# Attention steps in two runs of key tiles, with the next projection and the transposed maxima in front of the last values

## The chip, the cores and the metric

The kernel runs on one core of a Trainium2 chip. The metric is the time of one execution on the device in microseconds (us). A step below is one pair of heads against one block of 512 queries; there are 16.

## What is computed

One decoder block over 2048 rows of 256: a recurrent layer, cross attention against 1601 context rows with 8 heads of 64, and a mixture of 16 experts with a shared one, each followed by a normalisation of the rows. The change touches only the attention:

```
q = (x @ Wq).reshape(b, n, HEADS, DIM_HEAD)      # k, v likewise from the context
scores = einsum('bhnd,bhmd->bhnm', q, k) * scale
attn = softmax(scores, axis=-1)
out = einsum('bhnm,bhmd->bhnd', attn, v).reshape(b, n, HIDDEN)
x = layernorm(x + out @ Wo + bo)
```

## The kernel before

`attention` works through 4 chunks of 512 queries (`CHUNKS`), each with 4 pairs of heads (`PAIRS`): step `S` is chunk `S // 4`, pair `S % 4`. The 1601 keys are 13 tiles (`KT`), the last of 65.

For each tile, `score` on TensorE makes the scores of both heads, keys on partitions, in one of two PSUM buffers `st`. It takes four parts, each one matmul for each head: three products of high and low halves of Q and K, and a fourth that adds the negated row maxima (`ones_r` against `M`). The heads lie on partitions 0 to 63 and 64 to 127 of the operands. ScalarE's `exp` (L630) turns the buffer into a tile of `probs` in SBUF, a ring of `RING` places. GpSimd adds the 13 tiles to `accG` (L607). `values` (L816) multiplies a tile of probabilities with V and accumulates in the bank `av`; `sums` (L833) adds `accG` over its partitions into the bank `misc`; `copy_av` moves `av` to `o_raw`, and VectorE's `divide` in four parts (L689 and L691) makes `oT`.

The row maxima of a step are found one step ahead. `q_proj(S+1)` (L761) projects into `misc`, ScalarE's `q_high` and VectorE's `q_low` split it, and 26 pieces (`PIECES`, 13 for each head) of queries against keys go to the banks `mx[0]` and `mx[1]` (L780), one for each head. VectorE reduces each piece (L674; the two short ones of 66 keys L671); piece n waits until the reduction of piece n-2 has emptied its bank. `all_maxima` joins them in `nm`, `max_transpose` (L749) turns them into `mx[1]`, and VectorE's `max_rows` (L659) writes `M`.

At the first step of a chunk, `output` multiplies the last chunk's `oT` with Wo in two halves of 16 matmul passes (L847), `residual` adds x, and in the step behind it `statistics`, GpSimd's `inverse` and ScalarE's `norm` (L640) normalise.

Each engine runs its instructions in the order in which they are written out, and waits only on semaphores. TensorE's order in a step is: transpose of the maxima, projection for the next step, then three rounds of a run of tiles (`RUNS`: 0 to 4, 5 to 8, 9 to 12) and a group of values (`VALUES`: 0 to 2, 3 to 8, 9 to 12). The sums of the step before stand behind the first run. A tile has four slots of scores; `PIECE_AT` says for tiles 1 to 12 in which of then five slots the piece of head 0 and that of head 1 stand. The last pair of pieces (`LATE_PAIR`) stands inside the last group of values, in front of tile 10. `DIVIDE_AFTER` says behind which piece VectorE makes each of the four divides, `SHORT` which pair of pieces is the short one.

Of the kernel before, what the change touches and what calls it, by code (L numbers as in the profile page):

```python
# [13 lines left out]
S, D = 2048, 256  # L14
# [4 lines left out]
KT = (KEYS + P - 1) // P  # L19
# [3 lines left out]
PAIRS = HEADS // 2  # L23
QC = 512
CHUNKS = S // QC
QT = QC // P
# [9 lines left out]
def before_attention(nc, io, mem):  # L36
# [5 lines left out]
    with ExitStack() as ctx:  # L42
# [322 lines left out]
        def _(pe):  # L365
# [81 lines left out]
PIECES = 2 * PIECE_PAIRS  # L447
# [1 line left out]
DIVS = 4  # L449
LAST_V = (3, 5, 7, 9, 11, 12)  # L450
G_ADDS = KT - 1
RUNS = (range(0, 5), range(5, 9), range(9, KT))
HIGH, LOW_QUERY, LOW_KEY, MAXIMA = range(4)
VALUES = (range(0, 3), range(3, 9), range(9, KT))
PIECE_AT = {1: (0, 1), 2: (1, 2), 3: (2, 3), 4: (3, 4), 5: (0, 1), 6: (1, 2), 7: (2, 3), 8: (3, 4),
            9: (0, 1), 10: (0, 1), 11: (1, 2), 12: (2, 3)}
SHORT = 8
LATE_PAIR = 10
DIVIDE_AFTER = (8, 8, 16, 16)
SEEN = {3: 4, 5: 6, 7: 8, 9: 10, 11: 12}  # L460
NORM_AFTER = 4
RING = 8


def at_least(engine, semaphore, count):
# [5 lines left out]
def attention(nc, io, mem):  # L471
# [12 lines left out]
    with ExitStack() as ctx:  # L484
# [124 lines left out]
        @block.scalar  # L609
        def _(act):  # L610
            def q_high(F):
                act.wait_ge(p_q, F)
                at_least(act, p_qk, 2 * (F - 1) * KT)
                act.activation(Q_hi[F % 2][:], misc[:], ACT.Copy).then_inc(a_hi, 1)

            def exp(S, t):
                g, r = S * KT + t, rows_of(t)
                act.wait_ge(p_qk, 2 * (g + 1))
                if g >= RING:
                    act.wait_ge(p_pv, g - RING + 1)  # L620
                    before, old = divmod(g - RING, KT)
                    if before == STEPS - 1:
                        if old in LAST_V:
                            act.wait_ge(v_add, LAST_V.index(old) + 1)
                        else:
                            alone = [k for k in range(1, KT) if k not in LAST_V]
                            act.wait_ge(g_add, before * G_ADDS + alone.index(max(old, 1)) + 1)
                    else:
                        act.wait_ge(g_add, before * G_ADDS + max(old, 1))
                act.activation(probs[0:r, place(S, t)], st[g % 2][0:r, :], ACT.Exp, scale=DH ** -0.5).then_inc(a_probs, 1)  # L630

            def copy_av(S):
                act.wait_ge(p_pv, (S + 1) * KT)
                at_least(act, v_o, S * DIVS)
                act.activation(o_raw[:], av[:], ACT.Copy).then_inc(a_av, 1)

            def norm(c):
                act.wait_ge(g_shift3, c + 1)
                for i in range(QT):
                    act.activation(x1[:, i], x1[:, i], ACT.Identity, bias=shift3[:, i:i + 1], scale=rstd3[:, i:i + 1]  # L640
                                   ).then_inc(a_x2, 1)

            for S in range(STEPS):
                c, p = divmod(S, PAIRS)
                if S > 0:
                    copy_av(S - 1)
                if S + 1 < STEPS:
                    q_high(S + 1)
                for t in range(KT):
                    exp(S, t)  # L650
                    if p == 1 and t == NORM_AFTER and c > 0:
                        norm(c - 1)
            copy_av(STEPS - 1)

        @block.vector
        def _(dve):
            def max_rows(S):
                dve.wait_ge(p_mT, S + 1)
                dve.tensor_tensor(M[:].rearrange("p (i q) -> p i q", i=QT), mx[1][:, 0:P].unsqueeze(1).to_broadcast([P, QT, P]),  # L659
                                  mask[:].unsqueeze(2).to_broadcast([P, QT, P]), ALU.mult).then_inc(v_mT, 1)  # L660

            def q_low(F):
                dve.wait_ge(a_hi, F)
                dve.tensor_tensor(Q_lo[F % 2][:], misc[:], Q_hi[F % 2][:].bitcast(F32), ALU.subtract).then_inc(v_lo, 1)
# [42 lines left out]

            dve.tensor_tensor(mask[:], ident[:, 0:QT], ident[:, DH:DH + QT], ALU.add).then_inc(v_mask, 1)
            dve.wait_ge(v_mask, 1)
            for S in range(STEPS):  # L710
                c, p = divmod(S, PAIRS)
                max_rows(S)
                if p == 1 and c > 0:
                    statistics(c - 1)
                if S + 1 < STEPS:
                    q_low(S + 1)
                    for n in range(1, PIECES + 1):
                        piece_maximum(S + 1, n)
                        for i, at in enumerate(DIVIDE_AFTER):
                            if n == at and S > 0:  # L720
                                divide(S - 1, i)
                        if n == PIECES - 2 and p == 0 and c > 0:
                            residual(c - 1, 0, misc)
                            residual(c - 1, 1, misc)
                    all_maxima(S + 1)
                    if p == 0 and c > 0:
                        residual(c - 1, 2, mx[0])
                        residual(c - 1, 3, mx[0])
            for i in range(DIVS):
                divide(STEPS - 2, i)  # L730
            for n, t in enumerate(LAST_V):
# [14 lines left out]
        def _(pe):  # L746
# [4 lines left out]
            def q_proj(F):  # L751
                c, pair = divmod(F, PAIRS)
                at_least(pe, v_o, (F - 2) * DIVS)
                if pair == 2 and c > 0:
                    pe.wait_ge(v_r, (c - 1) * QT + 2)
                if F == 1:
                    pe.wait_ge(d_wq, 16)
                if pair == 0:
                    pe.wait_ge(d_x1Tc, c * 16)
                for k in range(DK):  # L760
                    mm = pe.matmul(misc[:], wq[:, k, pair * P:(pair + 1) * P], x1T[:, k, :],  # L761
                                   start=(k == 0), stop=(k == DK - 1))
                mm.then_inc(p_q, 1)

            def piece(F, n):

                i, j = piece_of(n)
                h, (k0, kn) = (n - 1) % 2, MC[j]
                rows = slice(DH * h, DH * h + DH)
                if n == 1:  # L770
                    pe.wait_ge(a_hi, F)
                    c, p = divmod(F - 1, PAIRS)
                    if p == 1 and c > 0:
                        pe.wait_ge(v_r, c * QT)
                if n <= 2:
                    at_least(pe, v_mx, (F - 2) * PIECES + PIECES - 2 + n)
                if n > 2:
                    pe.wait_ge(v_mx, (F - 1) * PIECES + n - 2)
                for a, q in enumerate(range(QT) if i is None else (i,)):
                    mm = pe.matmul(mx[h][:, a * kn:(a + 1) * kn], Q_hi[F % 2][rows, q * P:(q + 1) * P],  # L780
                                   K_hi[rows, F % PAIRS, k0:k0 + kn], start=True, stop=True)
                mm.then_inc(p_mx, 1)
# [54 lines left out]
            def output(c, half):  # L837

                if half == 0:
                    pe.wait_ge(d_wo, 16)  # L840
                    pe.wait_ge(v_o, (c + 1) * PAIRS * DIVS)
                else:
                    pe.wait_ge(v_mx, ((c + 1) * PAIRS + 1) * PIECES)
                bank = (misc, mx[0])[half]
                for i in (2 * half, 2 * half + 1):
                    for p in range(PAIRS):
                        mm = pe.matmul(bank[:, (i % 2) * D:(i % 2 + 1) * D], oT[:, p, i * P:(i + 1) * P], wo[:, p, :],  # L847
                                       start=(p == 0), stop=(p == PAIRS - 1))
                    mm.then_inc(p_wo, 1)
# [13 lines left out]
                        mm.then_inc(p_wo, 1)  # L863

            pe.wait_ge(g_ones, 4)
            for S in range(STEPS):
                c, p = divmod(S, PAIRS)
                ahead = S + 1 < STEPS
                max_transpose(S)
                if ahead:  # L870
                    q_proj(S + 1)
                n = 1
                for run, given in zip(RUNS, VALUES):
                    for t in run:
                        tile(S, t, n if ahead and t in PIECE_AT else None)
                        n += 2 if t in PIECE_AT else 0
                    if run is RUNS[0] and S > 0:
                        sums(S - 1)
                    if run is RUNS[-1] and p == 0 and c > 0:
                        output(c - 1, 0)  # L880
                    for t in given:
                        if t == LATE_PAIR and ahead:
                            piece(S + 1, n)
                            piece(S + 1, n + 1)
                        values(S, t)
                if p == 0 and c > 0:
                    output(c - 1, 1)
            last_output(False)
            sums(STEPS - 1)
            last_output(True)  # L890
# [803 lines left out]
```

## Time and profile before

| | us |
|---|---|
| median of 3 runs | 941.9 |
| lowest and highest | 939.98, 943.53 |
| the profiled execution | 938.92 |
| its span | 937.1 |
| first score of step 0 | 114.72 |
| transpose of step 1, of step 15 | 144.25, 617.24 |
| last values of step 15 done, output begins | 644.74 |

The attention takes 114.72 to 644.74, 530 us of the span; in front of it are the first layer and the keys and values, behind it the experts. In a row of the timeline the first number is the start in us from the span's start, the second the duration of the row, and xN is how many like instructions are merged in it: with N over 1 the duration runs from the first one's start to the last one's end. PE is TensorE's matmul, PEld its weight load, DVE VectorE, ACT ScalarE, POOL GpSimd. Matmuls are pipelined, so the start of the next one, not a duration, tells the pace. An f32 product with the full height of the array is made in two passes, which are counted one by one.

### The profile page before, as it was taken

The page shows a single profiled execution, that of the slowest core. Times are in us where ns is not written, and L with a number is a line of the kernel's source. Part 1 is how long each engine was busy: PE and PEld are TensorE (multiplying, and loading weights), DVE is VectorE, ACT ScalarE, POOL GpSimd, SP SyncE. Part 2 cuts the span into 40 slices and gives each one's busy share as a digit, 9 for nine tenths or more (in the row PEclk, how much of TensorE's full clock was granted, in tenths as well). Part 3 has the DMA queues.
Part 4 walks back from the last instruction along what each step waited for, and adds up shares of the span by engine and source line. Part 5 has one row for each costly group of instructions (what it writes and reads, how often), then busy time and mean ns, then how long its engine had stood idle before and what let it go on. Part 6 is the DMA issues. An engine that isn't in the chain of part 4 may idle for free. (4 is left out here: it accounts for less than half of the span.)

```text
span 937.1 us, 12963 instructions
## 1 busy us (share of the span) xinstructions
PE 891.1 (95%) x4616; PEld 527.6 (56%) x4616; DVE 551.5 (59%) x1123; ACT 351.8 (38%) x493; POOL 593.3 (63%) x397
## 2 busy tenths in 40 slices
PE   6998799999999999999999999998899999989993
PEld 3655355545555555565554564544678888855551
DVE  2898557667747767757766756754645121145552
ACT  2245144434525544435443434451441121123332
POOL 0454198898878889869889869882114400047785
PEclk9999899999999999999999999999999999999997
DMA  8013300000001000001000001040795100423210
GB/s 277 27 50 111 109 1 1 23 1 1 1 1 45 24 1 1 1 1 46 23 1 0 2 1 45 1 157 1 197 351 193 54 14 22 135 90 111 81 39 15
DMA packets 42873, 52.86 MB, mean 56 GB/s; under 512 B 4400, under 2 KB 33856, under 8 KB 42816
## 3 DMA queue, kind: packets, MB, share of 16 engines
q1 hardware_dynamic: 35808, 44.21, 14.8%
q0 software_dynamic: 3744, 6.32, 2.1%
q10 hardware_dynamic: 3264, 1.57, 0.6%
q8 instruction: 36, 0.59, 0.3%
q14 instruction: 21, 0.17, 0.1%
HBM read 38.42 MB, written 17.59 MB: 60 GB/s over the span
## 5 line engine op out<-in xcount | busy, mean ns | idle before, releaser
L607 POOL TENSOR_TENSOR accG<-accG,probs 128x1024 f32<-128x1024 f32 (+1 forms) x170 | 405.2, 2384 | 38.5 <-ACT probs L630 23.4
L630 ACT ACTIVATE probs<-st 128x1024 f32<-128x1024 f32 (+1 forms) x208 | 212.7, 1026 | 202.9 <-PE st L794 197.3
L674 DVE TENSOR_REDUCE mxp<-mx 128x1 f32<-128x512 f32 x360 | 231.9, 686 | 60.0 <-PE mx L780 54.6
L816 PE MATMUL av<-probs,V 128*64 128x512 f32 (+1 forms) x832 | 191.7, 598 | 0.0
L780 PE MATMUL mx<-K_hi,Q_hi 64*128 64x512 f32 (+1 forms) x480 | 137.9, 380 | 0.0
L816 PEld LDWEIGHTS av<-probs,V 128*64 128x64 f32 (+1 forms) x832 | 55.4, 136 | 105.7 <-issue 83.9
L794 PE MATMUL st<-Q_hi,K_hi 64*128 64x512 f32 (+1 forms) x416 | 113.0, 445 | 0.9 <-ACT probs L630 0.9
L780 PEld LDWEIGHTS mx<-K_hi,Q_hi 64*128 64x128 f32 x480 | 73.8, 184 | 52.0 <-issue 26.8
L794 PE MATMUL st<-M,ones_r 64*128 64x512 f32 (+1 forms) x416 | 101.1, 392 | 0.0
L794 PE MATMUL st<-Q_hi,K_lo 64*128 64x512 f32 (+1 forms) x416 | 96.7, 392 | 0.0
L794 PE MATMUL st<-Q_lo,K_hi 64*128 64x512 f32 (+1 forms) x416 | 94.5, 394 | 0.0
L794 PEld LDWEIGHTS st<-Q_hi,K_hi 64*128 64x128 f32 (+1 forms) x416 | 48.3, 180 | 47.0 <-ACT probs L630 30.5
L689 DVE RECIPROCAL misc<-misc 128x128 f32<-128x128 f32 x64 | 61.4, 960 | 13.5 <-PE misc L833 13.5
L1560 PE MATMUL bgu<-w_gate_up,xsT 128*128 x124 | 58.4, 594 | 1.0 <-ACT xsT L1456 1.0
L1177 DVE TENSOR_TENSOR hT<-hT,bu 128x512 f32<-128x512 f32 x32 | 22.0, 687 | 61.8 <-ACT hT L1090 57.5
L1295 PE MATMUL bt<-wd,hT 128*128 128x256 f32 x256 | 56.3, 380 | 0.4 <-DVE x L1186 0.4
L1090 ACT ACTIVATE hT<-bg 128x512 f32<-128x512 f32 x32 | 19.1, 597 | 99.4 <-PE bu L1280 97.2
L607 POOL TENSOR_TENSOR accG<-probs 128x1024 f32<-128x1024 f32 x16 | 38.3, 2395 | 27.9 <-ACT probs L630 27.9
L794 PEld LDWEIGHTS st<-M,ones_r 64*128 64x128 f32 (+1 forms) x416 | 50.9, 181 | 7.2 <-DVE M L659 0.3
L1295 PEld LDWEIGHTS bt<-wd,hT 128*128 128x128 f32 x256 | 48.5, 190 | 7.4 <-DVE x L1186 0.8
L1398 POOL MEMSET mhalf<- 128x2 f32 x1 | 0.1, 99 | 82.9 <-POOLq L914 82.9
L794 PEld LDWEIGHTS st<-Q_lo,K_hi 64*128 64x128 f32 (+1 forms) x416 | 49.6, 182 | 3.7
(198 smaller groups left out, 1238.0 us busy)
## 6 DMA issues: line engine op xcount, KB each, us to landing
w_gate_up<-in_gate_up SPq DMA_DIRECT2D x4, 2048.0 KB, 20.1
w_down<-in_down SPq DMA_DIRECT2D x2, 2048.0 KB, 15.8
xs<-scratch_sorted_x SPq DMA_DIRECT2D x31, 128.5 KB
scratch_sorted_x<-zero SPq DMA_DIRECT2D x7, 514.0 KB, 8.3
xT<-in_xT SPq DMA_DIRECT2D x4, 512.0 KB, 6.7
xring<-in_x SPq DMA_DIRECT2D x4, 512.0 KB, 8.7
scratch_x1b<-xT SPq DMA_DIRECT2D x4, 512.0 KB, 2.9
x<-scratch_x1b SPq DMA_DIRECT2D x4, 512.0 KB, 4.3
```

Source lines behind the costliest of these rows:

```text
L607: pool.tensor_tensor(total[0:r], so_far[0:r], probs[0:r, place(S, t)], ALU.add).then_inc(g_add, 1)
L630: act.activation(probs[0:r, place(S, t)], st[g % 2][0:r, :], ACT.Exp, scale=DH ** -0.5).then_inc(a_probs, 1)
L674: dve.tensor_reduce(mxp[:, F % 2, h * QT + i, j:j + 1], mx[h][:, 0:kn], AX.X, ALU.max).then_inc(v_mx, 1)
L689: dve.reciprocal(misc[:, cols], misc[:, cols]).then_inc(v_rsum, 1)
L780: mm = pe.matmul(mx[h][:, a * kn:(a + 1) * kn], Q_hi[F % 2][rows, q * P:(q + 1) * P], K_hi[rows, F % PAIRS, k0:k0 + kn], start=True, stop= ...
L794: mm = pe.matmul(st[g % 2][0:r, h * QC:(h + 1) * QC], w, q, start=(part == 0), stop=(part == MAXIMA))
L816: mm = pe.matmul(av[h * DH:(h + 1) * DH, :], V[0:r, t, (2 * p + h) * DH:(2 * p + h + 1) * DH], probs[0:r, place(S, t), h * QC:(h + 1) * QC ...
L1090: act.activation(hT[:, f], bg[f % 2][:], ACT.Silu).then_inc(a_silu, 1)
L1177: dve.tensor_tensor(hT[:, f], hT[:, f], bu[f % 2][:], ALU.mult).then_inc(v_h, 1)
L1295: mm = pe.matmul(bt[i % 2][:, 0:D], hT[:, f, i * P:(i + 1) * P], wd[:, f, :], start=(f == 0), stop=(f == FK - 1))
L1398: pool.memset(mhalf4[:], -0.5).then_inc(g_c4, 1)
L1560: mm = pe.matmul(bgu[r % 2][:], xsT[:, r, k * P:(k + 1) * P], w_gate_up[:, bass.ds(e * DK + k, 1), :].squeeze(1), start=(k == 0), stop=(k ...
```

## The change

The three runs of tiles become two, 0 to 6 and 7 to 12, and the three groups of values become two, 0 to 4 and 5 to 12. The ring has twelve places instead of eight. Every tile, tile 0 too, holds a pair of pieces; in tiles 4 to 6 both stand in the fifth slot. The late pair inside the values is gone, and the short pair stands in tile 9. The projection, now for step S+2, and the transpose, now for step S+1, stand behind the second run and in front of the last group of values; for step 0 and 1 they stand ahead of the loop. Both halves of the output product follow the transpose, the first into `mx[0]`, the second into `misc`. ScalarE splits Q behind the exponentials of a step, and then copies `av`; VectorE makes the low part and `M` behind the maxima and the residual behind them, and all four divides after piece 14. Piece 2 of a step now waits for `M` to be written.

```diff
-RUNS = (range(0, 5), range(5, 9), range(9, KT))
+RUNS = (range(0, 7), range(7, KT))
-VALUES = (range(0, 3), range(3, 9), range(9, KT))
-PIECE_AT = {1: (0, 1), 2: (1, 2), 3: (2, 3), 4: (3, 4), 5: (0, 1), 6: (1, 2), 7: (2, 3), 8: (3, 4),
-            9: (0, 1), 10: (0, 1), 11: (1, 2), 12: (2, 3)}
-SHORT = 8
-LATE_PAIR = 10
-DIVIDE_AFTER = (8, 8, 16, 16)
+VALUES = (range(0, 5), range(5, KT))
+PIECE_AT = {0: (0, 1), 1: (1, 2), 2: (2, 3), 3: (3, 4), 4: (4, 4), 5: (4, 4), 6: (4, 4),
+            7: (0, 1), 8: (1, 2), 9: (2, 3), 10: (2, 3), 11: (3, 4), 12: (3, 4)}
+SHORT = 9
+DIVIDE_AFTER = (14, 14, 14, 14)
-RING = 8
+RING = 12
@@ ScalarE
+            q_high(1)
             for S in range(STEPS):
-                if S > 0:
-                    copy_av(S - 1)
-                if S + 1 < STEPS:
-                    q_high(S + 1)
                 for t in range(KT):
                     exp(S, t)
                     if p == 1 and t == NORM_AFTER and c > 0:
                         norm(c - 1)
-            copy_av(STEPS - 1)
+                if S + 2 < STEPS:
+                    q_high(S + 2)
+                copy_av(S)
@@ VectorE
+            max_rows(0)
+            q_low(1)
+            for S in range(STEPS - 1):
                 c, p = divmod(S, PAIRS)
                 if p == 1 and c > 0:
                     statistics(c - 1)
+                for n in range(1, PIECES + 1):
+                    piece_maximum(S + 1, n)
+                    for i, at in enumerate(DIVIDE_AFTER):
+                        if n == at and S > 0:
+                            divide(S - 1, i)
+                all_maxima(S + 1)
+                if S + 2 < STEPS:
+                    q_low(S + 2)
+                max_rows(S + 1)
+                if p == 0 and c > 0:
+                    for i in range(QT):
+                        residual(c - 1, i, (mx[0], misc)[i // 2])
@@ TensorE
             def q_proj(F):
-                if pair == 2 and c > 0:
-                    pe.wait_ge(v_r, (c - 1) * QT + 2)
             def piece(F, n):
+                if n == 2:
+                    pe.wait_ge(v_mT, F)
             def output(c, half):
                 if half == 0:
+                    pe.wait_ge(v_mx, ((c + 1) * PAIRS + 1) * PIECES)
                 else:
-                    pe.wait_ge(v_mx, ((c + 1) * PAIRS + 1) * PIECES)
-                bank = (misc, mx[0])[half]
+                    pe.wait_ge(v_lo, (c + 1) * PAIRS + 2)
+                bank = (mx[0], misc)[half]
+            max_transpose(0)
+            q_proj(1)
             for S in range(STEPS):
-                max_transpose(S)
-                if ahead:
-                    q_proj(S + 1)
                 for run, given in zip(RUNS, VALUES):
                     for t in run:
+                        tile(S, t, n if ahead else None)
                     if run is RUNS[0] and S > 0:
                         sums(S - 1)
-                    if run is RUNS[-1] and p == 0 and c > 0:
-                        output(c - 1, 0)
+                    if run is RUNS[-1]:
+                        if S + 2 < STEPS:
+                            q_proj(S + 2)
+                        if ahead:
+                            max_transpose(S + 1)
+                        if p == 0 and c > 0:
+                            output(c - 1, 0)
+                            output(c - 1, 1)
                     for t in given:
-                        if t == LATE_PAIR and ahead:
-                            piece(S + 1, n)
-                            piece(S + 1, n + 1)
                         values(S, t)
-                if p == 0 and c > 0:
-                    output(c - 1, 1)
```

## Rows read from the trace of the kernel before

**Rows 1.** Busy time by engine of steps 1 to 14 (busy us and instructions of each).

```profile
core 0: us, PE busy (x) PEld busy (x) DVE busy (x) ACT busy (x) POOL busy (x), PEclk, DMA share, GB/s
...
144.25:617.24 472.99, 472.99 (x2856) 253.50 (x2855) 323.69 (x554) 209.26 (x222) 403.74 (x181) 1.00 0.04 13
```

**Rows 2.** Table of waits of the attention: total us, times, longest.

```profile
ACT probs L630 <- PE st L794: 197.3, 159, 5.9
...
PEld st L794 <- ACT probs L630: 30.5, 103, 0.7
...
PEld mx L780 <- DVE mxp L674: 19.6, 60, 0.8
```

**Rows 3.** TensorE's timeline in step 6, from transpose to transpose: start, us.

```profile
312.60 0.33 PE L749 MATMUL mx<-ident,nm 128*128 128x128 f32 x1
...
314.58 0.51 PE L794 MATMUL st<-Q_hi,K_hi 64*128 64x512 f32 x2
...
319.51 0.50 PE L794 MATMUL st<-Q_hi,K_hi 64*128 64x512 f32 x2
...
320.86 1.08 PE L833 MATMUL misc<-accG,ones 128*64 128x512 f32 x4
...
324.44 0.50 PE L780 MATMUL mx<-K_hi,Q_hi 64*128 64x512 f32 x1
...
329.79 5.37 PE L816 MATMUL av<-probs,V 128*64 128x512 f32 x24
...
335.09 0.29 PE L780 MATMUL mx<-K_hi,Q_hi 64*128 64x66 f32 x1
...
336.57 0.39 PE L780 MATMUL mx<-K_hi,Q_hi 64*128 64x512 f32 x1
...
340.64 1.08 PE L816 MATMUL av<-probs,V 128*64 128x512 f32 x4
...
344.81 0.33 PE L749 MATMUL mx<-ident,nm 128*128 128x128 f32 x1
```

**Rows 4.** The same timeline, inside tiles 2 and 3.

```profile
317.97 0.40 PE L794 MATMUL st<-M,ones_r 64*128 64x512 f32 x2
...
318.66 0.39 PE L780 MATMUL mx<-K_hi,Q_hi 64*128 64x512 f32 x1
...
319.04 0.49 PE L780 MATMUL mx<-K_hi,Q_hi 64*128 64x512 f32 x1
```

**Rows 5.** VectorE's timeline, single reductions of the same tiles.

```profile
318.30 0.68 DVE L674 TENSOR_REDUCE mxp<-mx 128x1 f32<-128x512 f32 x1
...
319.09 0.69 DVE L674 TENSOR_REDUCE mxp<-mx 128x1 f32<-128x512 f32 x1
...
319.70 0.68 DVE L674 TENSOR_REDUCE mxp<-mx 128x1 f32<-128x512 f32 x1
```

**Rows 6.** ScalarE's timeline: an exponential of step 6, a normalisation of step 9.

```profile
318.43 1.02 ACT L630 ACTIVATE probs<-st 128x1024 f32<-128x1024 f32 x1 [0.41 <-PE st L794]
...
425.89 2.06 ACT L640 ACTIVATE x<-x,shift,rstd 128x256 f32<-128x256 f32 x4
```

**Rows 7.** VectorE's timeline: the first two divides of step 6.

```profile
321.99 0.96 DVE L689 RECIPROCAL misc<-misc 128x128 f32<-128x128 f32 x1
...
323.19 0.96 DVE L689 RECIPROCAL misc<-misc 128x128 f32<-128x128 f32 x1
```

**Rows 8.** TensorE's timeline: transposes around output step 8, second half of its output.

```profile
377.02 0.33 PE L749 MATMUL mx<-ident,nm 128*128 128x128 f32 x1
...
412.91 3.72 PE L847 MATMUL mx<-wo,oT 128*128 128x256 f32 x16
...
416.47 0.27 PE L749 MATMUL mx<-ident,nm 128*128 128x128 f32 x1
...
448.81 0.33 PE L749 MATMUL mx<-ident,nm 128*128 128x128 f32 x1
```

**Rows 9.** GpSimd's timeline: the first add of step 7.

```profile
350.31 2.40 POOL L607 TENSOR_TENSOR accG<-probs 128x1024 f32<-128x1024 f32 x1 [1.47 <-ACT probs L630]
```

**Rows 10.** Weight loads in the page's list of instruction groups: busy, mean ns.

```profile
L794 PEld LDWEIGHTS st<-Q_hi,K_hi 64*128 64x128 f32 (+1 forms) x416 | 48.3, 180 | 47.0 <-ACT probs L630 30.5
```

More of the change, by code:

```diff
@@ L709, in _ @@
             dve.wait_ge(v_mask, 1)
-            for S in range(STEPS):
+            max_rows(0)
+            q_low(1)
+            for S in range(STEPS - 1):
                 c, p = divmod(S, PAIRS)
-                max_rows(S)
                 if p == 1 and c > 0:
                     statistics(c - 1)
[L715 to L725, printed above, removed]
-                    if p == 0 and c > 0:
-                        residual(c - 1, 2, mx[0])
-                        residual(c - 1, 3, mx[0])
+                for n in range(1, PIECES + 1):
[10 more added lines that the diff above has]
+                        residual(c - 1, i, (mx[0], misc)[i // 2])
             for i in range(DIVS):
@@ L874, in _ @@
                     for t in run:
-                        tile(S, t, n if ahead and t in PIECE_AT else None)
-                        n += 2 if t in PIECE_AT else 0
+                        tile(S, t, n if ahead else None)
+                        n += 2
                     if run is RUNS[0] and S > 0:
                         sums(S - 1)
-                    if run is RUNS[-1] and p == 0 and c > 0:
-                        output(c - 1, 0)
+                    if run is RUNS[-1]:
[6 more added lines that the diff above has]
+                            output(c - 1, 1)
                     for t in given:
-                        if t == LATE_PAIR and ahead:
-                            piece(S + 1, n)
-                            piece(S + 1, n + 1)
                         values(S, t)
-                if p == 0 and c > 0:
-                    output(c - 1, 1)
             last_output(False)
```

## The prediction, made blind

> **What bounds the kernel now.** The change touches only the attention stage, so I read its steps 1 to 14 as one window first [rows 1]: of 472.99 us TensorE is busy for all, VectorE for 323.69 (68%), GpSimd for 403.74 (85%), ScalarE for 209.26 (44%), and TensorE has its full granted clock (1.00). The limit is TensorE's own order of work, and busy time cannot tell how much of it is waiting, since a matmul's record covers its pipeline. The table of waits does [rows 2]: the scores' weight loads waited 103 times for an exponential, the maxima's 60 times for VectorE's reduction. These come in tenths of a microsecond and are what the change trades in.
>
> TensorE's timeline of one plain step shows where it goes [rows 3]. From one transpose to the next, 312.60 to 344.81, are 32.21 us. The three runs of tiles take 6.28 (314.58 to 320.86), 5.35 (324.44 to 329.79) and 5.55 (335.09 to 340.64), together 17.18. The rest is 15.03: transpose and projection 1.98, sums with three tiles of values 3.58, six tiles of values 5.30, and the last group with the late pair of maxima pieces 4.17. Two groups of one kind give the law of a values group: six units in 5.30 against four (sums counted as one) in 3.58 is 0.86 a unit and 0.14 for both edges.
>
> Inside a run a tile is four or five slots of 0.23 us (the fifth tile: 319.51 to 320.86, 1.35, is five slots of 0.2325, 0.10 for a wait ahead of it and 0.09 for the edge behind), in each of which both heads' half-height matmuls run side by side, so five slots are 1.16. The tiles really come at 1.26 to 1.40. Three loops stretch them, each read from rows:
> - ScalarE: an exponential starts 0.46 after the last score slot of its tile (317.97 to 318.43), and the tile after the next, which takes its buffer, can start 1.08 after that (319.51) [rows 3, 4, 6].
> - VectorE: a reduction starts 0.43 after its piece (318.66 to 319.09), the next one 0.605 later (319.70), and the piece that reuses a bank 0.74 after the reduction's start (318.30 to 319.04) [rows 4, 5].
> - A matmul behind such a wait, or behind an edge of a run, shows 0.10 more (0.49 to 0.51 for 0.39 to 0.40) [rows 3, 4].
>
> Carrying these numbers from slot to slot through the step as it stands, each head's half of the array on its own, gives tile starts of 1.99, 3.02, 4.33, 5.59, 6.90 for run one (rows: 1.98, then 6.91 for the fifth), runs of 17.29 for 17.18 and a step of 32.15 for 32.21. So the same walk may be made for the new order, good to about 0.1 a run.
>
> **The change part by part.**
> *Groups and edges.* Outside the runs a step of after has: sums and five tiles of values, 0.86 x 6 + 0.14 = 5.30; projection and transpose, 1.98 less its edge into a tile, 1.94 with the entry; eight tiles of values, 0.86 x 8 + 0.14 = 7.02. Together 14.26, against 15.03: a gain of 0.77. Of it 0.59 is the late pair, which costs 4.17 - (4 x 0.86 + 0.14) now, and the rest the edges of one values group.
>
> *Pieces.* That pair now sits in a tile, and tile 0 has pieces too, so all 13 tiles have five slots (tile 9 takes the short piece, which costs 0.2: its tile now takes 335.09 to 336.57, 0.2 over five slots and an edge [rows 3]).
>
> *Runs.* The walk for the first run, from its start: 0, 1.26, 2.57, 3.88, 5.14, 6.54, 7.94, values at 9.69. Tiles 2 and 3 wait for exponentials: with the last score slot fifth, two tiles take 0.10 + 0.93 + 0.46 + 1.08 = 2.57. Only the first two tiles of a run are free of this, because both buffers stand empty; three runs have six such tiles, two have four. Tiles 4 to 6 have both pieces in the fifth slot. There VectorE is late: the second head's reduction can't start before 0.43 + 0.605 after the first head's piece, and the next second-head piece not before another 0.74, 1.775 in all, where the tiles would come at 1.16 (1.40 from tile 3, whose first piece is a slot earlier). The walk has waits of 0.38, 0.13 and 0.15 there. Second run, from its start: 0, 1.26, 2.58, 4.12, 5.50, 6.76, values at 8.50, with waits for VectorE of 0.29 in tile 8 and 0.27 in tile 12. Together 18.19; less the 0.1 by which the walk overstates the present runs, 18.1. That is 0.9 more than now.
>
> *Net of a step:* +0.9 - 0.77 = +0.13 us; over the 15 steps with pieces +2.0. The last step has no pieces: one more wait for an exponential (0.3) against one pair of edges (0.24) and the transposed maxima waiting ready; I put it at 0.
>
> *Divides.* All four come after piece 14. A divide takes 1.20 (321.99 to 323.19), the first starts 1.13 behind the sums (320.86) [rows 3, 7]: 9.69 + 1.13 + 4.80 = 15.62, while the second run's first piece is issued at 14.95. Its reduction is late by 0.24, and tile 8's wait of 0.29 is that; it is in the walk.
>
> *Projection and transpose in front of the last values.* The same passes on TensorE. ScalarE's rounding of Q and VectorE's low part move beside the eight tiles of values, where both idle; queued behind them are the output copy on ScalarE, and residual and statistics on VectorE, all wanted later. New is that the transpose stands close behind the last piece: its maxima are ready about 1.0 after the last piece's reduction starts, 24.46 by the walk, and the projection ahead of it lasts until 25.18. It costs nothing while VectorE is under 0.7 later.
>
> *Output steps.* Steps 4, 8 and 12 take 39.45 (377.02 to 416.47), 32.21 plus 7.24, and sixteen of its 32 matmuls take 3.56 with their entry (412.91 to 416.47) [rows 8]; behind the transpose, with no entry, all 32 are 6.9, so 0.3 comes off each. The step after them takes 32.34 (to 448.81), 0.13 over a plain one, because statistics hold VectorE at its start; they now fit beside values: 0.13 off each. Together -1.3. Normalisation (2.06 [rows 6]) now stands between exponentials 4 and 5 with the run going on, but nothing before tile 7 wants exponential 5: nothing, and at the worst 1 us three times.
>
> *Twelve places.* Nothing now waits for a place: ScalarE's waits are for scores (197.3 us [rows 2]), and GpSimd starts a step's adds after 1.47 us idle, each of the twelve taking 2.4 [rows 9], 29 of the 32 us. So the places only permit the two runs, and GpSimd would bind only below 29 us a step.
>
> *Sum:* +2.0 - 1.3 = +0.7. The profiled execution has 938.92 (span 937.1), 3 below the median of the runs, 941.9; the difference carries over: 942.6.
>
> **The rivals.**
> 1. *Tiles keep today's pace (faster).* If VectorE's lateness in the fifth slot is absorbed, tiles run at today's mean for those with pieces, 1.31 (the present second run, 5.35 less its edge, over four): 13 x 1.31 + 0.2 + 0.2 for the short piece and the edges = 17.4 for 18.1, 0.65 x 15 = 9.8 less: 933. For it: the head whose piece waits holds only its half of the array. Against: the reduction loop's 1.775 is from rows and the walk already lets the halves slip.
> 2. *The block of divides holds the second run (slower).* It decides when the last divide ends more than 0.9 behind the first piece of the second run (0.67 in the walk): then the lag doesn't drain and tiles alternate at the loop of both heads, 2.95 for two (1.775 + 1.17), 1.47 for 1.36: 0.11 x 6 x 15 = 9.9 more, 952.5. For it: nothing shows four divides in a row next to pieces. Against: the reductions need only 1.21 a tile.
> 3. *The transpose waits for its maxima.* If the last reduction is 1.4 late rather than 0.27, its slack of 0.72 is gone and TensorE idles 0.4 a step, 6 in all: 948.5. For it: the second run ends with VectorE behind. Against: the walk ends with most of the slack left.
> 4. *Edges cost a whole weight load.* If at a change between half and full height of the array a load of 0.18 [rows 10] lies bare and not 0.10 of it, each of the four edges that fall away (two of the late pair, two of a group) gives 0.08 more: 0.08 x 4 x 15 = 4.8, 938. The rows speak against it: the first score behind an edge is longer by 0.11 (0.51 for 0.40 [rows 3, 4]). The Trainium skill, in "TensorE: Matmul & The Clock Gate", section "The mechanism", has the rule behind this rival: a weight load overlaps running matmuls only when its row group differs. By that rule the whole load would be bare, and the rows agree with a part of it only.
>
> **How the numbers follow.** Forecast 0.55 (942.6, its own range 938 to 947.5), rival 1 0.22, rival 2 0.12, rival 3 0.07, rival 4 0.04. A measurement of this kernel tells 0.5% (4.7 us) from no change. Faster (below 937.2): rival 1, half of rival 4, a tail of 0.03 of the forecast: 0.27. Slower (above 946.6): rival 2, most of rival 3, a tail of 0.02: 0.20. Same: 0.53. The range leaves out the far half of rival 1 and of rival 2: 933.5 to 950.5. The unknown costs lie inside it: 0.1 a run in the walk is 3, the normalisation up to 3.
>
> **What would show it.** Plain steps between transposes at 32.3 to 32.4; first run 9.6 to 9.7 and second 8.4 to 8.5; tiles 4 to 6 at 1.4 or more with pieces waiting for VectorE, whose waits rise well above 19.6 us; late-pair waits gone; output steps near 39.1. A plain step of 31.6 with tiles at 1.31 is rival 1; second runs of 9 us, rival 2; a gap in front of the transpose, rival 3. The forecast is wrong if a run's length differs from the walk by over 0.3.

## The result and the profile after

| | us |
|---|---|
| median before, 20 runs | 941.18 |
| median after, 20 runs | 947.52 |
| ratio | 1.0070, 95% interval 1.0058 to 1.0081 |
| profiled execution after: span | 944.5 (937.1 before) |

The change makes the kernel 0.7% slower, 6.3 us. The forecast was 942.6, no change, with a range of 933.5 to 950.5. The time lies inside the range, on its slow side, but above 946.6, where the prediction lets slower begin, for which it had a chance of 0.20.

TensorE's timeline after from the transpose for step 6 to the one for step 7, at the starts of tiles, sums, values, projection and transpose (start, us; compare [rows 3]). The 32 passes behind the first transpose are the last values of step 5:

```profile
310.19 0.27 PE L746 MATMUL mx<-ident,nm 128*128 128x128 f32 x1
310.39 7.09 PE L813 MATMUL av<-probs,V 128*64 128x512 f32 x32
317.41 0.49 PE L777 MATMUL mx<-K_hi,Q_hi 64*128 64x512 f32 x1
...
318.67 0.40 PE L791 MATMUL st<-Q_hi,K_hi 64*128 64x512 f32 x2
...
319.98 0.51 PE L791 MATMUL st<-Q_hi,K_hi 64*128 64x512 f32 x2
...
321.36 0.50 PE L791 MATMUL st<-Q_hi,K_hi 64*128 64x512 f32 x2
...
322.62 0.43 PE L791 MATMUL st<-Q_hi,K_hi 64*128 64x512 f32 x2
...
323.60 0.83 PE L777 MATMUL mx<-K_hi,Q_hi 64*128 64x512 f32 x2
323.93 0.73 PE L791 MATMUL st<-Q_hi,K_hi 64*128 64x512 f32 x2
...
325.37 0.49 PE L791 MATMUL st<-Q_hi,K_hi 64*128 64x512 f32 x1
...
327.18 1.08 PE L830 MATMUL misc<-accG,ones 128*64 128x512 f32 x4
328.09 4.46 PE L813 MATMUL av<-probs,V 128*64 128x512 f32 x20
332.49 0.50 PE L777 MATMUL mx<-K_hi,Q_hi 64*128 64x512 f32 x1
...
340.94 1.98 PE L756 MATMUL misc<-x1T,wq 128*128 128x512 f32 x4
342.76 0.27 PE L746 MATMUL mx<-ident,nm 128*128 128x128 f32 x1
```

From transpose to transpose are 32.57 us, 32.21 before. The first run takes 9.77 (317.41 to 327.18), the second 8.45 (332.49 to 340.94), sums with five tiles of values 5.31, projection and the way to the values 2.02, eight tiles of values 7.02. The row of 323.60 is the pair of pieces in the fifth slot of tile 4: two matmuls that could run side by side in 0.39 take 0.83, since the second waits. The table of waits says for whom (total us, times, longest; compare [rows 2]):

```profile
DVE mxp L672 <- PE mx L777: 106.7, 84, 5.6
...
PEld mx L777 <- DVE mxp L672: 35.3, 105, 0.4
...
PEld st L791 <- ACT probs L629: 18.0, 54, 0.7
```

Pieces waited 105 times for a reduction, 35.3 us, where it had been 60 times and 19.6. VectorE itself stood idle for 106.7 us waiting for pieces, so it is not short of time. Most of that is one long wait a step while TensorE multiplies the last values (VectorE's timeline of the same step):

```profile
317.94 2.68 DVE L672 TENSOR_REDUCE mxp<-mx 128x1 f32<-128x512 f32 x4 [5.63 <-PE mx L777]
```

Fifteen such waits are about 82 us; the other 25 or so are short ones inside the runs, where in turn pieces wait for VectorE.

The four divides and the reductions around them (VectorE's timeline of the same step; compare [rows 7]):

```profile
328.31 0.97 DVE L687 RECIPROCAL misc<-misc 128x128 f32<-128x128 f32 x1 [0.16 <-PE misc L830]
...
332.90 0.29 DVE L689 TENSOR_TENSOR oT<-o_raw,misc 128x128 f32<-128x128 f32 x1
333.11 2.58 DVE L672 TENSOR_REDUCE mxp<-mx 128x1 f32<-128x512 f32 x4
```

The first reduction behind them starts 0.62 after its piece (332.49).

Two places cost once. In step 0 the first piece, now in tile 0, waits for the first rounding of Q; in step 14, where no projection stands ahead of it, the transpose waits for its maxima:

```profile
115.84 0.49 PE L777 MATMUL mx<-K_hi,Q_hi 64*128 64x512 f32 x1 [0.69 <-ACT Q_hi L613]
...
616.46 0.33 PE L746 MATMUL mx<-ident,nm 128*128 128x128 f32 x1 [1.01 <-DVE nm L676]
```

So the time went here. Transposes 1 to 14 are 444.20 apart (140.43 to 584.63), 3.44 more than the 440.76 before: seven plain steps at +0.36, the three with output at 39.48 for 39.43, the three behind them at 32.57 for 32.35. Step 0 costs 0.7 at its start and 0.3 more in its length; steps 14 and 15 together 1.3. That is 5.8 of the 7.4 by which the two spans differ. 0.4 lies ahead of the stage, and 1.2 behind it, where TensorE's clock was granted at a mean of 0.77 of full speed between 663 and 681 us, against 0.91 in the stretch of the same work before (657 to 675). In both it had the lower of its two levels, 1.2 GHz, from 661.1 us on, after TensorE had stood several times for 0.5 to 1.5 us between the last output products and behind them; it came back at 664.5 before and at 671.3 after. A kernel with the old order, e12 below, was granted 0.78 over the same work (658.6 to 676.6), so this difference can't be put down to the change.

### The profile page after: what moved, and what is told of

It is laid out like the page before. It is cut to its first block and busy times, and to the rows that moved or that the text cites. A ratio compares the mean times of both kernels' runs of the same rounds, so it can differ in the third digit from the quotient of the medians.

```text
span 944.5 us, 12926 instructions
## 1 busy us (share of the span) xinstructions
PE 896.9 (95%) x4616; PEld 535.0 (57%) x4616; DVE 551.2 (58%) x1123; ACT 351.4 (37%) x493; POOL 593.1 (63%) x397
## 5 line engine op out<-in xcount | busy, mean ns | idle before, releaser
L672 DVE TENSOR_REDUCE mxp<-mx 128x1 f32<-128x512 f32 x360 | 231.6, 685 | 113.0 <-PE mx L777 106.7
L813 PE MATMUL av<-probs,V 128*64 128x512 f32 (+1 forms) x832 | 184.9, 594 | 0.0
L777 PE MATMUL mx<-K_hi,Q_hi 64*128 64x512 f32 (+1 forms) x480 | 153.8, 387 | 0.8 <-ACT Q_hi L613 0.7
L813 PEld LDWEIGHTS av<-probs,V 128*64 128x64 f32 (+1 forms) x832 | 58.3, 137 | 116.2 <-issue 115.2
L777 PEld LDWEIGHTS mx<-K_hi,Q_hi 64*128 64x128 f32 x480 | 78.0, 184 | 67.6 <-DVE mxp L672 35.3
L791 PE MATMUL st<-M,ones_r 64*128 64x512 f32 (+1 forms) x416 | 109.5, 396 | 0.0
L791 PE MATMUL st<-Q_hi,K_lo 64*128 64x512 f32 (+1 forms) x416 | 109.5, 400 | 0.0
L791 PEld LDWEIGHTS st<-M,ones_r 64*128 64x128 f32 (+1 forms) x416 | 59.6, 181 | 7.0
L791 PEld LDWEIGHTS st<-Q_hi,K_lo 64*128 64x128 f32 (+1 forms) x416 | 55.0, 180 | 7.5
L791 PEld LDWEIGHTS st<-Q_hi,K_hi 64*128 64x128 f32 (+1 forms) x416 | 44.4, 179 | 24.4 <-ACT probs L629 18.0
L634 ACT ACTIVATE o_raw<-av 128x512 f32<-128x512 f32 x16 | 9.6, 598 | 126.0 <-PE av L813 126.0
```

The source lines that it names most:

```text
L672: dve.tensor_reduce(mxp[:, F % 2, h * QT + i, j:j + 1], mx[h][:, 0:kn], AX.X, ALU.max).then_inc(v_mx, 1)
L791: mm = pe.matmul(st[g % 2][0:r, h * QC:(h + 1) * QC], w, q, start=(part == 0), stop=(part == MAXIMA))
L813: mm = pe.matmul(av[h * DH:(h + 1) * DH, :], V[0:r, t, (2 * p + h) * DH:(2 * p + h + 1) * DH], probs[0:r, place(S, t), h * QC:(h + 1) * QC ...
```

## The experiments

Each kernel was run beside the kernel before on the same chip, and the ratio is to it. There were three such groups, on three chips, in which the kernel before took 938.89 (e1 to e4), 940.94 (e5 to e8) and 939.76 us (e9 to e12), so ratios compare better than medians. The experiments have 4 to 12 executions each. The plain step is the distance of two transposes in a step without output; within one profiled execution such distances differ by up to 0.09 (a single one of 35.43 in e4 is left out).

| kernel | median us | ratio, 95% | plain step | expected step |
|---|---|---|---|---|
| before | 941.18 | 1 | 32.21 | |
| after | 947.52 | 1.0070 (1.0058 to 1.0081) | 32.57 | 32.34 |
| e1_three_runs | 941.64 | 1.0030 (1.0017 to 1.0043) | 32.33 | 32.3 |
| e9_three_places | 943.5 | 1.0035 (1.0023 to 1.0046) | 32.32 | 32.35 |
| e2_spaced | 929.72 | 0.9903 (0.9883 to 0.9922) | 31.57 | 31.55 |
| e3_divides | 965.71 | 1.0275 (1.0251 to 1.0299) | 33.97 | 32.65 |
| e4_walk_places | 967.84 | 1.0317 (1.0296 to 1.0339) | 34.05 | 31.4 |
| e7_after_half | 927.12 | 0.9853 (0.9820 to 0.9886) | 31.33 | 31.5 |
| e8_before_half | 932.5 | 0.9912 (0.9885 to 0.9938) | 31.72 | 31.7 |
| e6_before_spaced | 938.08 | 0.9970 (0.9954 to 0.9986) | 32.05 | 31.9 |
| e5_three_spaced | 934.38 | 0.9931 (0.9908 to 0.9953) | 31.68 | 31.2 |
| e12_before_ring12 | 941.2 | 1.0006 (0.9991 to 1.0020) | 32.21 | 32.2 |
| e10_spaced_ends | 930.32 | 0.9889 (0.9872 to 0.9905) | 31.57 | 31.55 |
| e11_short8 | 928.72 | 0.9873 (0.9857 to 0.9890) | 31.51 | 31.4 |

### Is it the merging of the runs?

```diff
-RUNS = (range(0, 7), range(7, KT))
+RUNS = (range(0, 5), range(5, 9), range(9, KT))
-VALUES = (range(0, 5), range(5, KT))
+VALUES = (range(0, 3), range(3, 9), range(9, KT))
-PIECE_AT = {0: (0, 1), 1: (1, 2), 2: (2, 3), 3: (3, 4), 4: (4, 4), 5: (4, 4), 6: (4, 4),
-            7: (0, 1), 8: (1, 2), 9: (2, 3), 10: (2, 3), 11: (3, 4), 12: (3, 4)}
+PIECE_AT = {0: (0, 1), 1: (1, 2), 2: (2, 3), 3: (3, 4), 4: (3, 4), 5: (0, 1), 6: (1, 2),
+            7: (2, 3), 8: (3, 4), 9: (0, 1), 10: (1, 2), 11: (2, 3), 12: (3, 4)}
-DIVIDE_AFTER = (14, 14, 14, 14)
+DIVIDE_AFTER = (10, 10, 18, 18)
```

> The change with its merging of runs undone: three runs (0 to 4, 5 to 8, 9 to 12), three groups of values (0 to 2, 3 to 8, 9 to 12), two divides each after pieces 10 and 18, no tile with both pieces in the fifth slot. Projection and transpose stay in front of the last values, every tile keeps its pair of pieces, the ring stays at 12. My theory (two runs save 0.28 us a step in edges but lose more, because only four tiles instead of six start on empty score buffers and because tiles 4 to 6 hit the reduction loop): the walk gives a step of 32.05 against 32.33 for the changed kernel, so a plain step of 32.3 where the changed kernel has 32.57, and about 943.5 us, 4 below the changed kernel. Rival (the merged edges are a gain, and the loss comes from the projection and transpose in front of the values): the step rises by 0.2 to 0.3 over 32.57 and the time is 951.

The step was 32.33, 0.24 under that of after, and the time 0.4% lower, as the walk had it. The rival, that the merged edges are a gain in this order, falls. But this kernel undoes two things, the merging and the three tiles with both pieces in the fifth slot (divides and some other pieces move with the runs). A kernel with the second alone tells them apart:

```diff
-4: (4, 4), 5: (4, 4), 6: (4, 4),
+4: (3, 4), 5: (3, 4), 6: (3, 4),
```

> The changed kernel with only tiles 4, 5 and 6 altered: head 0's piece in the fourth slot, head 1's in the fifth, instead of both in the fifth. It prices that one choice. My theory: the walk gives 32.10 for 32.33, so a plain step of 32.35 for 32.57 and 3.5 us less than the changed kernel, about 0.35% above the kernel before. Rival (the four tiles that no longer start on empty buffers are what costs): no change against the changed kernel within 1 us.

32.32 and 1.0035: the same gain, 0.25 a step, from these three tiles. So these tiles are enough for the whole difference of e1, and two runs against three, with pieces one slot apart in both, is a draw. That the edges saved and the tiles that start on empty buffers cancel is how the walk explains the draw; no run separates the two.

### Is it the loop of pieces and reductions?

```diff
# e7, e8: the reduction of a whole piece
-mx[h][:, 0:kn], AX.X, ALU.max)
+mx[h][:, 0:kn // 2], AX.X, ALU.max)
```

> The changed kernel, where VectorE reduces only the first half of the columns of each whole piece (256 of 512, so half of the keys is left out of the row maxima of steps 1 to 15). TensorE does the same work. A reduction then holds VectorE about 0.27 us less. My theory (the changed order loses to the loop of pieces and reductions): the walk gives a step of 31.25 for 32.33, so a plain step of 31.5 for 32.57 and 16 us less than the changed kernel, 931 to 933. Rival (the tiles are held by ScalarE's two buffers and by having fewer fresh starts): the step falls by under 0.4 and the time stays above 941.

> The kernel before with the same edit (half of the keys left out of the maxima of steps 1 to 15). My theory: the same loop costs the old order less than half as much, the walk gives 31.66 for 32.15, so 7.5 us less than before, about 933: with cheap reductions the old order is no better than the new one or a little worse. Rival (the loop is no more in the one order than in the other): both lose the same.

Cheaper reductions take 1.24 us off a step of after and 0.49 off one of before. In e7 nothing on TensorE waits for the reduction of a piece any more; what comes up instead is ScalarE's loop, and GpSimd, for which TensorE waited neither before nor after (table of waits of e7_after_half):

```profile
PEld st L791 <- ACT probs L629: 33.5, 100, 0.6
...
ACT probs L629 <- POOL accG L606: 7.5, 14, 0.7
...
PEld misc L830 <- POOL accG L606: 1.7, 7, 0.3
```

With the loop weakened in both, the changed order is ahead, 31.33 to 31.72. So with reductions this short the changed order gains 0.39 a step, for which the saved edges and the absorbed late pair are the reason that the prediction gives, and the full reductions take 0.75 more of the changed order than of the old one. 1.24 is more than the 1.08 that was expected.

The same loop can be served instead of shortened: a second reduction starts 0.605 after the first [rows 5], so the two pieces of a tile should stand that far apart, two or three slots.

```diff
# e2, on after
+PIECE_AT = {t: (1, 4) for t in range(KT)}
# e6, on before
+PIECE_AT = {t: (1, 4) for t in range(1, KT)}
```

> The changed kernel with one line other: in all 13 tiles the piece of head 0 stands in the second slot and that of head 1 in the fifth (instead of side by side or one slot apart). My theory (the loss is the loop of pieces and reductions: a second reduction starts 0.605 us after the first, so pieces should stand two or three slots of 0.23 apart): the walk gives 31.3 a step for 32.33, so a plain step of 31.55 and about 932 us, 1% below the kernel before. Rival (ScalarE's loop with two score buffers sets the tiles' pace anyway, and the reductions are only late where they are not needed): the step stays above 32.3 and the time above 943.

> The kernel before with one line other: in tiles 1 to 12 the piece of head 0 in the second slot and that of head 1 in the fifth. The projection stays at the head of the step, the late pair in the values. My theory: spacing helps here too, but less, since its places kept pieces a slot further on from tile to tile: the walk gives 31.87 for 32.15, 4.3 us less, ratio 0.9955. Rival (spacing helps only together with pieces in every tile): no change within 0.2%.

In e2 the step is 31.57, where 31.55 was expected, and the kernel is 1% faster than before. TensorE's timeline at the head of its step 7:

```profile
342.77 0.50 PE L790 MATMUL st<-Q_hi,K_hi 64*128 64x512 f32 x2
343.11 0.39 PE L776 MATMUL mx<-K_hi,Q_hi 64*128 64x512 f32 x1
...
343.81 0.39 PE L776 MATMUL mx<-K_hi,Q_hi 64*128 64x512 f32 x1
344.04 0.40 PE L790 MATMUL st<-Q_hi,K_hi 64*128 64x512 f32 x2
344.28 0.50 PE L776 MATMUL mx<-K_hi,Q_hi 64*128 64x512 f32 x1
...
345.08 0.42 PE L776 MATMUL mx<-K_hi,Q_hi 64*128 64x512 f32 x1
345.31 0.49 PE L790 MATMUL st<-Q_hi,K_hi 64*128 64x512 f32 x2
```

The pieces stand 0.70 and 0.80 apart, and VectorE takes the 14 of a run in one row without a gap that the profile shows; the waits for it are down to a third of after's, and those for exponentials to half (9.1 for 18.0):

```profile
343.53 9.25 DVE L671 TENSOR_REDUCE mxp<-mx 128x1 f32<-128x512 f32 x14 [5.87 <-PE mx L776]
```

```profile
PEld st L790 <- issue: 26.7, 32, 1.5
...
PEld mx L776 <- DVE mxp L671: 11.9, 45, 0.3
PEld st L790 <- ACT probs L628: 9.1, 24, 0.7
```

In the old order the same places give 0.16 a step and 0.3%, less than the 0.28 expected. Its rival, no change within 0.2% without pieces in every tile, is not excluded by the times (the interval ends at 0.9986); the step of 32.05 for 32.21 speaks against it.

The sum of waits in the table is not what they cost: e9 has 120 waits and 34.2 us for reductions, nearly what after has, and its step is 0.25 shorter.

### The block of divides

```diff
-DIVIDE_AFTER = (14, 14, 14, 14)
+DIVIDE_AFTER = (14, 14, 20, 20)
```

> The changed kernel with two divides after piece 14 and two after piece 20 instead of four after 14. My theory (the block of four costs next to nothing, since the reductions catch up in the second run): the walk gives +0.07 a step, so 948 within 1.5 us. Rival (the block of divides holds the second run, rival 2 of the prediction): the second run gets shorter by 0.3 or more, 943 or less.

The expectation failed by far: 965.71. Not the block costs, but two divides inside a run. TensorE in tile 11 of step 5, and VectorE at that time:

```profile
312.99 0.40 PE L791 MATMUL st<-Q_hi,K_lo 64*128 64x512 f32 x2
314.49 0.50 PE L777 MATMUL mx<-K_hi,Q_hi 64*128 64x512 f32 x1 [1.11 <-DVE mxp L672]
```

```profile
311.37 0.95 DVE L687 RECIPROCAL misc<-misc 128x128 f32<-128x128 f32 x1
...
313.55 0.29 DVE L689 TENSOR_TENSOR oT<-o_raw,misc 128x128 f32<-128x128 f32 x1
313.76 3.85 DVE L672 TENSOR_REDUCE mxp<-mx 128x1 f32<-128x512 f32 x6
```

TensorE stands for 1.11 us in every step from 1 to 14. Both halves of the array stand: the piece is head 0's, and the score of head 1 that follows it in the order needs nothing from VectorE, yet starts with it (314.50 behind 314.49).

```profile
314.50 0.72 PE L791 MATMUL st<-M,ones_r 64*128 64x512 f32 x2
```

The walk had an error: it took VectorE's time for divides at ends of runs only, where a group of values covers them. I worked it out again after the run: with the divides where they stand it gives 33.6, +1.27 over after, and +1.40 was measured. The same error spoilt the next kernel, whose places had been searched with it:

```diff
+PIECE_AT = {0: (0, 0), 1: (0, 3), 2: (0, 2), 3: (2, 4), 4: (2, 4), 5: (3, 4), 6: (4, 4),
+            7: (0, 2), 8: (0, 3), 9: (0, 3), 10: (1, 3), 11: (1, 4), 12: (3, 4)}
+SHORT = 5
+DIVIDE_AFTER = (14, 14, 20, 20)
```

> The changed kernel with the places of pieces, the short pair (tile 5) and the divides (two after piece 14, two after 20) that came out best of a search over the same walk. My theory: the walk gives 31.17 a step for 32.33, so a plain step of 31.4 and about 930 us. Rival (the walk is only good near the orders it was fitted to): the step is off the walk by more than 0.4, above 31.8, and the time above 936.

967.84. TensorE stands at the same place, behind the divides in the run, 14 times and for 27.0 us in all. The mended walk gives 33.35 for it, 1.02 over after; 34.05 was measured, 1.48 over it. The difference is not explained.

### Two runs or three, once the pieces are spaced

```diff
# e5: runs, values and divides of e1, and
+PIECE_AT = {0: (0, 0), 1: (0, 2), 2: (0, 3), 3: (0, 3), 4: (4, 4), 5: (0, 3), 6: (1, 4),
+            7: (1, 3), 8: (2, 4), 9: (0, 0), 10: (0, 2), 11: (0, 2), 12: (3, 3)}
```

> The changed order with three runs and three groups of values as before, divides after pieces 10 and 18, and the places of pieces that came out best of a search over the walk with all divides at ends of runs. The walk gives 30.95 against 31.31 for the two runs with pieces spaced in all tiles: a plain step of 31.2 for 31.53 there, and about 925 us. It also tells whether two runs or three are better once the pieces are spaced. Rival (the merged edges are a gain once VectorE is out of the way): at or above 930.

31.68 and 934.38, not 31.2 and 925: the walk had TensorE, ScalarE and VectorE in it, but not GpSimd. Its table of waits:

```profile
PEld misc L829 <- POOL accG L605: 5.5, 15, 0.4
...
PEld mx L745 <- DVE nm L675: 5.4, 15, 1.8
```

In every step the sums, which stand behind the first run of five tiles, wait 0.37 for GpSimd's adds of the step before, and the transpose waits for its maxima, 0.36 on average. In e2, with seven tiles ahead of the sums, they wait for no add. Its step is 0.11 shorter, but the intervals of the two ratios overlap, the two have different places of pieces as well as different runs, and no run had the places of e2 in three runs. So it is not shown that two runs are the better order once the pieces are spaced.

### Places, and the two ends

```diff
# e12, on before
-RING = 8
+RING = 12
```

> The kernel before with twelve places for probabilities instead of eight and nothing else. Theory: no exponential waits for a place, so no change, within 0.2%. Rival (hidden waits on GpSimd's adds behind the scores' waits): a gain of 0.3% or more.

1.0006: no change. The places only permit the two runs.

```diff
# e10, on e2
+    places = (3, 4) if S == 0 and t == 0 else PIECE_AT[t]
-                        if ahead:
+                        if S + 2 < STEPS:
                             max_transpose(S + 1)
                     for t in given:
                         values(S, t)
+                        if S == STEPS - 2 and t == given[1] and run is RUNS[-1]:
+                            max_transpose(S + 1)
# e11, on e10
-SHORT = 9
+SHORT = 8
```

> The spaced kernel of before (pieces in the second and fifth slot of every tile) with its two single losses taken away: in step 0 tile 0 has its pieces in the fourth and fifth slot, so they don't wait for the first rounding of Q, and in step 14, where no projection stands ahead of the transpose, the transpose comes behind the second tile of values. Theory: the transpose of step 15 waited 1.0 us and the first piece about 0.4, so 1.4 us less than the spaced kernel, ratio to before 0.989. Rival (other work ends last there): no change.

> The same with the short pair of pieces in tile 8 instead of tile 9. The walk gives 31.18 for 31.31, so 2 us less, ratio 0.987. Rival (the walk's treatment of the short pieces is coarse): the step moves by under 0.05 or up.

In e10 the wait of the last transpose is gone, and step 14, from first score to first score, takes 29.95 for 30.93 in e2:

```profile
599.48 1.94 PE L816 MATMUL av<-probs,V 128*64 128x512 f32 x8
601.35 0.33 PE L745 MATMUL mx<-ident,nm 128*128 128x128 f32 x1
601.60 3.65 PE L816 MATMUL av<-probs,V 128*64 128x512 f32 x16
```

The other end gave nothing that the trace shows: step 0 takes 32.01 in e10 and 31.51 in e2. Part of that is the clock, which was at its lower level for the first 2.1 us of the step in e10 and for 1.5 in e2.

The ratios 0.9889 and 0.9873 are in the order expected, but their intervals overlap with each other's and with that of e2, so neither step is shown by its time; the step of e11 is 0.06 shorter, where 0.13 was expected. e11, 928.72 us, is the fastest kernel here that takes its maxima over all keys: 1.3% under the kernel before, 2% under the changed one.

## Why the prediction came out as it did

**The terms.** Outside the runs 14.26 was predicted for a step and 14.35 measured (5.31, 2.02, 7.02): the projection with its entries costs 0.08 more. The walk of the runs was close, 1.26, 2.57, 3.95, 5.21, 6.52, 7.96, 9.77 for 1.26, 2.57, 3.88, 5.14, 6.54, 7.94, 9.69 in the first and 8.45 for 8.50 in the second: 18.22 for 18.19. The step that failed is the one behind it, "less the 0.1 by which the walk overstates the present runs, 18.1": an error of the walk in one order, 17.29 for 17.18, was carried over to another as if it were a bias. It and the 0.08 make 0.2 a step, 3 us. So the sign that the prediction put on the plain step, 32.3 to 32.4, failed with 32.57, while its signs on the two runs came true.

**The steps with output** lost what was forecast: 0.3 and 0.13 off, against a plain step that is longer by 0.36, gives 39.5 and 32.57, and 39.48 and 32.57 were measured. The "near 39.1" among the signs doesn't follow from the prediction's own terms, which give 39.45 + 0.13 - 0.3 = 39.28.

**What was left out.** The two ends. Step 0: pieces in tile 0 put the first rounding of Q in front of the second slot, 0.7. Step 14 has no projection, which I had named as the cover of the transpose; nobody had asked what happens in the one step where that cover is missing. 1.0. With the 0.3 of step 0's length these are what stands between +0.7 and the measured +6.3, together with the 3 above; about 0.6 is not accounted for. Inside the profiled executions 1.2 of the difference lies behind the stage, as shown above. The last step itself came out level, 27.20 for 27.24, as put.

**The rivals.** Rival 1, tiles at today's pace, fell: the tiles with both pieces in one slot wait as the loop says. Its premise, that a waiting head holds only its half of the array, is wrong: in e3 head 1's score starts at 314.50 with head 0's piece of 314.49 and not before, though its own half stood free for a microsecond. A wait holds whatever follows it in the order, and the other half is ahead only by what was issued before. The walk, which had each half go on its own, shares this error; what it is worth there wasn't worked out. Rival 2, the block of divides, didn't come: 0.62 behind the first piece for 0.67 in the walk and 0.9 as the point. e3 shows that VectorE's lateness can cost 1.4 us a step, 21 in the stage of the profiled executions (19 by the ratios), but by divides inside a run. Rival 3 occurs once, in step 14; its repeated form is in e5. Rival 4: no run priced an edge by itself, but the first score behind one is 0.50 for 0.40 in after as it was [rows 3, 4]. The Trainium skill, "TensorE: Matmul & The Clock Gate", section "The mechanism", says that a weight load overlaps running matmuls only when it is for another row group. A gain of 0.32 a step by it was not there: outside the runs 14.35 was measured for 14.26.

**What is shown of the cause.** The change saves 0.39 a step when reductions are cheap (e7, e8) and loses 0.36 as it is, so 0.75 of its step are the reductions. Three tiles with both pieces in the fifth slot are 0.25 of that (e9). With the pieces three slots apart in all tiles another 0.75 goes (e2), 1.0 in all, where the old order gains 0.16 (e6). That the other 0.5 of the reductions' toll lies in pieces one slot apart fits this but is argued. How much of the 1.0 comes from ScalarE's side, since moved pieces also move the last score slot, was not separated; the waits for exponentials fell with it.

## What to carry to other kernels

Merging stages to save switches also takes away the places where the other engines catch up; price the loop inside the merged stage, not only the edges. A producer that feeds a slower consumer through two buffers should spread its pieces by the consumer's own time (0.605 us here), and work of the consumer that is due at any time belongs where the producer is busy with something else. When a step is covered by its neighbour, look for the first and last pass, where the neighbour is missing.

## What was not expected of the hardware

TensorE waited 35 us for VectorE in the changed kernel while VectorE stood idle for 107 us in front of pieces, some 25 of them between the tiles of a run: neither engine's busy share, 58% and 95%, shows that two engines wait for each other in turn. A matmul that waits for a semaphore stops the other half of the array too, as soon as the next instruction in the order is that half's: 1.11 us at one piece in e3. And GpSimd, in no wait of TensorE's before, appears in them in every step of 31.7 us with the sums early (e5), and now and then at 31.3 us with the sums late (e7), though its twelve adds need only 29 us. My reading is that what binds is where in the step its last add is asked for, not the sum of the adds.
